# Row sums divided with 32x32 block turns on VectorE, modulations over four column tiles, and a new written order

## What is computed

```
m  = silu(cond) @ w_ada + b_ada            # nine chunks: shift, scale, gate of S, X, M
x += gS * self_attention(ln(x)*(1+scS)+shS)          # S: 16 heads of 16
x += gX * top16_cross_attention(ln(x)*(1+scX)+shX, ctx)   # X: only the 16 largest scores
x += gM * swiglu(ln(x)*(1+scM)+shM)                  # M: 256 -> 2*1024 -> 256
ss = silu(cond) @ Wss + bss                # scale and shift of L (queries) and C (context)
x += cross_attention(ada_ln(x), ada_ln(ctx)) @ Wp + bp    # L
```

## Time and profile before

| what | us |
|---|---|
| runs of the kernel before | 675.61, 676.38, 676.73 |
| the profiled execution, its time | 675.24 |
| its span, first to last instruction | 673.4 |
| TensorE busy, matmuls | 629.7 |
| TensorE busy, weight loads | 544.9 |
| VectorE busy | 454.3 |
| ScalarE busy | 438.4 |
| GpSimd busy | 340.8 |

### The profile page before, as it was taken

One profiled execution on the slowest core, in us unless ns is written; L12 is line 12 of the kernel. 1 busy time (PEld: TensorE's weight loads), 2 busy tenths in 40 slices (PEclk: granted clock), 3 DMA queues, 4 the chain that ended last, 5 costly groups with the idle time before them and its releaser, 6 DMA issues.

```text
span 673.4 us, 21451 instructions
## 1 busy us (share of the span) xinstructions
PE 629.7 (94%) x7931; PEld 544.9 (81%) x7931; DVE 454.3 (67%) x2081; ACT 438.4 (65%) x1074; POOL 340.8 (51%) x613
## 2 busy tenths in 40 slices
PE   4979977999999999999999999999999999999985
PEld 4858865888888888888988888888887877989973
DVE  2262899949948739379395694966945999953241
ACT  1446674757867766767777775776768756846553
POOL 4172242567843655746457353564742454766620
PEclk9979988999999999999999999999999999999998
DMA  9921200010110110101011101101000000000000
GB/s 289 382 85 48 74 25 26 17 49 18 33 42 18 42 33 28 45 34 41 18 41 34 40 18 34 41 17 50 17 18 18 18 25 18 3 18 9 1 10 24
DMA packets 19637, 30.32 MB, mean 45 GB/s; under 512 B 1987, under 2 KB 11087, under 8 KB 19279
## 3 DMA queue, kind: packets, MB, share of 16 engines
q1 hardware_dynamic: 19424, 28.93, 13.7%
q10 hardware_dynamic: 111, 0.03, 0.0%
HBM read 26.75 MB, written 2.20 MB: 43 GB/s over the span
## 4 chain that ended last, share of the span: by engine, by line
PE 53%; DVE 36%; SPq 4%; issue 3%; ACT 3%; DMA 1%; POOL 0%; DVEq 0%; ACTq 0%; POOLq 0%
PE dense_bank L1076 8%; DVE arena L844 8%; DVE arena L856 7%; DVE top L840 5%; PE score_room L1003 5%; DVE next L852 5%; PE dense_bank L1028 5%; PE score_room L988 5%; PE dense_bank L1065 4%; PE dense_bank L962 4%; PE dense_bank L974 3%; PE dense_bank L1050 3%; PE dense_bank L1058 3%; PE dense_bank L977 3%; PE dense_bank L1037 2%
## 5 line engine op out<-in xcount | busy, mean ns | idle before, releaser
L679 ACT ACTIVATE probs<-score_room 128x1024 f32<-128x1024 f32 x96 | 97.6, 1032 | 44.7 <-PE score_room L1009 27.7
L1076 PE MATMUL dense_bank<-h_t_M,w_m 128*128 128x128 f32 x1024 | 124.7, 277 | 1.3 <-ACT h_t_M L626 1.3
L1076 PEld LDWEIGHTS dense_bank<-h_t_M,w_m 128*128 128x128 f32 x1024 | 119.4, 192 | 4.7 <-issue 2.1
L712 ACT ACTIVATE arena<-dense_bank,bias_cols 128x128 f32<-128x128 f32 x256 | 73.3, 378 | 34.7 <-PE dense_bank L1076 34.4
L575 POOL TENSOR_SCALAR arena<-arena 128x512 bf16<-128x512 f32 x64 | 39.6, 619 | 95.1 <-DVE arena L856 94.8
L566 POOL TENSOR_TENSOR x_in<-x_in,gated 128x256 f32<-128x256 f32 x48 | 34.8, 726 | 71.8 <-DVE gated L886 71.5
L856 DVE MATCH_REPLACE8 arena<-next,arena 128x128 f32<-128x128 f32 x256 | 67.7, 276 | 0.0
L844 DVE MATCH_REPLACE8 arena<-top,arena 128x128 f32<-128x128 f32 x256 | 67.7, 276 | 0.0
L886 DVE TENSOR_TENSOR gated<-dense_bank,gates 128x256 f32<-128x256 f32 x48 | 20.0, 419 | 69.3 <-PE dense_bank L1058 41.4
L840 DVE MAX8 top<-arena 128x8 f32<-128x128 f32 x256 | 55.1, 277 | 0.9 <-ACT arena L664 0.9
L852 DVE MAX8 next<-arena 128x8 f32<-128x128 f32 x256 | 55.0, 277 | 0.0
(11 more groups left out here) (158 smaller groups left out, 1510.1 us busy)
## 6 DMA issues: line engine op xcount, KB each, us to landing
gates<-gates_dram SPq DMA_DIRECT2D x48, 256.0 KB, 3.3
x_in<-in_x SPq DMA_DIRECT2D x16, 128.0 KB, 2.2
ctx_in<-in_ctx SPq DMA_DIRECT2D x16, 128.0 KB, 2.7
w_m<-in_L_xcond_w_m SPq DMA_DIRECT2D x1, 2048.0 KB, 14.8
out_y<-x_in SPq DMA_DIRECT2D x16, 128.0 KB, 1.7
arena<-in_L_xcond_w_ada SPq DMA_DIRECT2D x2, 768.0 KB, 9.5
w_m<-in_L_xcond_w_m SPq DMA_DIRECT2D x1, 1024.0 KB, 18.6
w_qkv<-in_L_xcond_w_qkv SPq DMA_DIRECT2D x1, 768.0 KB, 5.6
```

The lines of the kernel that those rows point to most:

```text
L679: nc.scalar.activation(probs[:, pair[0], 1024 * u:1024 * u + 1024], score_room[:, 1024 * u:1024 * u + 1024], ACT.Exp).then_inc(probs_ready, 1)
L712: e = nc.scalar.activation(dst[:, P * j:P * j + P], d[:, P * j:P * j + P], ACT.Identity, bias=bias_cols[:, col + j:col + j + 1])
L1076: e = nc.tensor.matmul(d[:, P * j:P * j + P], w_m1[:, c, at:at + P], h_t["M"][:, n % H_RING["M"], c], start=(c == 0), stop=(c == CK - 1))
```

## The change

Seven edits are made together.

1. The division moves onto VectorE. `o_out`, `sumturn`, `oturn` and `o_t_out` go. `scale k` now has five instructions: a turn of the 128x512 product in 32x32 blocks from PSUM to SBUF, the reciprocals, two multiplications, and a turn of the 128x256 quotient in 32x32 blocks into `o_t`. VectorE waits for its own result between them. `out k` waits for `scale k`. The bank of `value k` is free after the first of the five.
2. The modulations swap their operands: the conditions, padded to 32 columns, are the stationary operand, and the weights are streamed, 128 columns to each of four column tiles of the array. The result has conditions on partitions, so a copy on VectorE (`mods_copy`) and a turn on TensorE (`mods_turn`) follow ahead of `mods_out`.
3. TensorE runs 24 turns of the identity before it waits for the condition.
4. ScalarE waits for the condition and computes its tanh first, then issues its nine loads.
5. TensorE turns the bias rows after `mods S`, not ahead of it; the first two setup results lie in the last two banks.
6. VectorE clears the padding of the condition at the start with one more instruction.
7. All due times are new, and with them every engine's order and the banks.

The core of the diff (the table of due times, the semaphores and the wait counters are cut):

```diff
+WARM_TURNS = 24
...
-    **{f"value {a}": f"o_out {a}" for a in ATT}, **{f"sumturn {a}": f"scale {a}" for a in ATT},
-    **{f"oturn {a}": f"o_t_out {a}" for a in ATT},
+    **{f"value {a}": f"scale {a}" for a in ATT},
...
         @block.scalar
+            act.wait_ge(cond_loaded, 16)
+            nc.scalar.activation(cond_tanh, cond, ACT.Tanh, scale=0.5).then_inc(cond_step, 1)
             at = 0
...
                 act.dma_start(bias_rows[at:at + n, :], v.rearrange("(c p) -> c p", p=P)).then_inc(rows_loaded, 16)
...
-            act.wait_ge(cond_loaded, 16)
-            nc.scalar.activation(cond_tanh, cond, ACT.Tanh, scale=0.5).then_inc(cond_step, 1)
...
+                if name == "mods_copy":
...
+                    nc.vector.tensor_copy(mod_rows[:], dense_bank[DENSE[f"mods {of[0]}", 0][0]][:, 0:P]).then_inc(mods_copied, 1)
...
                 if name == "scale":
                     k = of[0]
-                    dve.wait_ge(sums_turned, nth(f"sumturn {k}", n))
-                    nc.vector.reciprocal(iv.rearrange("p c o g -> p (c o g)"),
-                                         d[:, :, :, :, D].rearrange("p c o g -> p (c o g)")).then_inc(inv_done, 1)
+                    d = dense_bank[DENSE[f"value {k}", n][0]]
+                    dve.wait_ge(value_done, nth(f"value {k}", n))
+                    nc.vector.transpose(o_turned[:].rearrange("p j b e -> p (j b e)"), d[:]).then_inc(o_taken, 1)
+                    dve.wait_ge(o_taken, nth(full, n))
+                    nc.vector.reciprocal(inv[:].rearrange("p j b -> p (j b)"),
+                                         o_turned[:].rearrange("p j b e -> p (j b) e")[:, :, D]).then_inc(inv_done, 1)
                     dve.wait_ge(inv_done, nth(full, n))
                     for c in range(CK):
...
+                            o_norm[:, c].rearrange("p b o e -> p o b e"), o_turned[:, 2 * c:2 * c + 2, :, 0:D],
+                            inv[:, 2 * c:2 * c + 2].unsqueeze(3).broadcast_to([P, 2, GROUPS, D]), ALU.mult)
+                    e.then_inc(o_normed, 1)
+                    dve.wait_ge(o_normed, nth(full, n))
+                    if n:
+                        dve.wait_ge(out_done, nth(f"out {k}", n - 1))
+                    nc.vector.transpose(o_t[:, ATT[k]].rearrange("p c t -> p (c t)"),
+                                        o_norm[:].rearrange("p c b o e -> p (c b o e)")).then_inc(o_t_ready, 1)
...
         @block.tensor
+            def mods_of(ln, d):
...
+                for c in range(CK):
+                    for j in range(4):
+                        e = nc.tensor.matmul(d[32 * j:32 * j + 32, 0:P], silu_t[:, c], cols[j][:, c],
+                                             start=(c == 0), stop=(c == CK - 1))
...
             pe.wait_ge(ident_ready, 1)
+            for t in range(WARM_TURNS):
+                nc.tensor.transpose(dense_bank[DENSE_BANKS - 1][:, 0:P], ident[:], ident[:])
             pe.wait_ge(cond_step, 3)
...
                 if name == "mods":
...
+                    mods_of(of[0], d).then_inc(mods_done, 1)
+                    if NTH[full, 0] == 0:
+                        pe.wait_ge(rows_loaded, 9 * 16)
+                        nc.tensor.transpose(dense_bank[DENSE_BANKS - 2][:, 0:NBIAS], bias_rows,
+                                            ident[0:NBIAS, 0:NBIAS]).then_inc(setup_turned, 1)
+                if name == "mods_turn":
+                    pe.wait_ge(mods_copied, nth(f"mods_copy {of[0]}", 0))
+                    nc.tensor.transpose(d[:, 0:P], mod_rows[:], ident[:]).then_inc(mods_turned, 1)
...
-                if name == "sumturn":
...
-                if name == "oturn":
...
-                        pe.wait_ge(o_t_ready, nth(f"o_t_out {k}", n))
+                        pe.wait_ge(o_t_ready, nth(f"scale {k}", n))
```

More of the change, by code:

```diff
@@ new lines @@
+    "mods_copy S": (845,),
+    "mods_turn S": (882,),
+    "mods_out S": (940,),
+    "mods C": (1000,),
+    "mods_copy C": (1105,),
+    "mods_turn C": (1142,),
+    "mods_out C": (1187,),
+    "mods X": (2028,),
+    "mods_copy X": (2133,),
+    "mods_turn X": (2689,),
+    "mods_out X": (2965,),
+    "mods M": (2801,),
+    "mods_copy M": (2910,),
+    "mods_turn M": (2947,),
+    "mods_out M": (3046,),
+    "mods L": (3308,),
+    "mods_copy L": (3438,),
+    "mods_turn L": (3527,),
+    "mods_out L": (3572,),
@@ new lines @@
+    "gate S": (1400,),
+    "gate_out S": (1605,),
+    "gate_store S": (1732,),
+    "gate_load S": (2182, 2232, 2282, 4408, 5329, 7675, 10386, 13881, 19337, 22589, 25289, 28296, 33533, 35500, 37457, 43719),
+    "gate X": (2103,),
+    "gate_out X": (2308,),
+    "gate_store X": (2435,),
+    "gate_load X": (2885, 2935, 2985, 8344, 11608, 13669, 17488, 21872, 25836, 29089, 33473, 34126, 39930, 42390, 43808, 49199),
+    "gate M": (2460,),
+    "gate_out M": (2578,),
+    "gate_store M": (2705,),
@@ L201 @@
+    "down": (10255, 13800, 15973, 19534, 23760, 28304, 31755, 36053, 38140, 43344, 46509, 48951, 52571, 56314, 57281, 59914),
[4 rows of a table added]
 }
 ON = {
-    "pe": ("mods", "gate", "outbias", "turn", "q", "kv", "score", "maxturn", "weigh", "value", "sumturn",
-           "oturn", "down", "out", "up"),
-    "dve": ("mods_out", "gate_out", "outbias_out", "stats", "rowmax", "split", "top", "rest", "scale", "gated"),
-    "act": ("mod", "q_out", "kv_out", "score_out", "max_out", "exp", "o_out", "o_t_out", "lin", "tanh", "lin_b"),
+    "pe": ("mods", "mods_turn", "gate", "outbias", "turn", "q", "kv", "score", "maxturn", "weigh", "value",
+           "down", "out", "up"),
@@ L207 @@
+    "dve": ("mods_copy", "mods_out", "gate_out", "outbias_out", "stats", "rowmax", "split", "top", "rest", "scale", "gated"),
+    "act": ("mod", "q_out", "kv_out", "score_out", "max_out", "exp", "lin", "tanh", "lin_b"),
     "pool": ("rstd", "norm", "pre", "add", "mask", "half", "silu", "glu"),
@@ L240 @@
 DENSE = rooms({
-    **{f"mods {ln}": f"mods_out {ln}" for ln in LNS}, **{f"gate {k}": f"gate_out {k}" for k in GATE},
+    **{f"mods {ln}": f"mods_copy {ln}" for ln in LNS}, **{f"mods_turn {ln}": f"mods_out {ln}" for ln in LNS},
+    **{f"gate {k}": f"gate_out {k}" for k in GATE},
     "outbias L": "outbias_out L", **{f"turn {ln}": f"mod {ln}" for ln in LNS},
@@ L373, in block_kernel @@
         mods_done = sem("mods_done")
+        mods_copied = sem("mods_copied")
+        mods_turned = sem("mods_turned")
         mods_ready = sem("mods_ready")
@@ L428, in block_kernel @@
                    "lin": lin_ready, "lin_b": lin_b_ready, "exp": probs_ready, "rowmax": max_done,
-                   "score_out": scores_out, "mask": mask_ready, "o_out": o_ready, "scale": o_norm_ready,
-                   "o_t_out": o_t_ready, "value": value_done}
+                   "score_out": scores_out, "mask": mask_ready, "scale": o_taken, "mods_copy": mods_copied,
+                   "value": value_done}
         block = ctx.enter_context(nc.Block())
@@ L680, in _ @@
                                          score_room[:, 1024 * u:1024 * u + 1024], ACT.Exp).then_inc(probs_ready, 1)
-                if name == "o_out":
-                    k = of[0]
-                    d = dense_bank[DENSE[f"value {k}", n][0]]
-                    if n:
-                        act.wait_ge(sums_turned, nth(f"sumturn {k}", n - 1))
-                    act.wait_ge(value_done, nth(f"value {k}", n))
-                    nc.scalar.copy(o_raw[:, ATT[k]].rearrange("p j t -> p (j t)"), d[:]).then_inc(o_ready, 1)
-                if name == "o_t_out":
-                    k = of[0]
-                    d = dense_bank[DENSE[f"oturn {k}", n][0]]
-                    if n:
-                        act.wait_ge(out_done, nth(f"out {k}", n - 1))
-                    act.wait_ge(o_turned, nth(f"oturn {k}", n))
-                    nc.scalar.copy(o_t[:, ATT[k]].rearrange("p c t -> p (c t)"), d[:, 0:C]).then_inc(o_t_ready, 1)
                 if name in ("lin", "lin_b"):
@@ L766, in _ @@
                 full = " ".join(part)
+                if name == "mods_copy":
+                    if NTH[full, 0]:
+                        dve.wait_ge(mods_turned, NTH[full, 0])
+                    dve.wait_ge(mods_done, nth(f"mods {of[0]}", 0))
+                    nc.vector.tensor_copy(mod_rows[:], dense_bank[DENSE[f"mods {of[0]}", 0][0]][:, 0:P]).then_inc(mods_copied, 1)
                 if name == "mods_out":
@@ L906, in _ @@
                     wait_empty(pe, DENSE[full, n])
+                    if DENSE[full, n][1] is None and DENSE[full, n][0] >= DENSE_BANKS - 2:
+                        pe.wait_ge(cols_ready, 1)
                 if (full, n) in SCORES:
@@ L909, in _ @@
                 if name == "mods":
-                    ln = of[0]
-                    pe.wait_ge(ada_loaded[ln], 16)
-                    if ln in "LC":
-                        w = ss_q if ln == "L" else ss_kv
-                        cols = [w[:, :, P * c:P * c + P] for c in range(4)]
-                    else:
-                        at = 3 * C * MOD[ln]
```

(22 more changed lines are left out.)

67 lines of the change are left out of this document (34 added, 33 removed), and 257 rows, old and new, of the table DUE.

## The result

The changed kernel takes 669.66 us (median of 8 runs, 667.88 to 674.82) against 676.48 (8 runs, 674.64 to 679.41): a ratio of 0.991, 95% interval 0.9885 to 0.9935. That is 0.9% faster where 5.4% was forecast; the time lies at the upper edge of the range. The profiled execution took 667.88 us with a span of 665.7.

The account below looks back on a forecast made before the run. TensorE was taken to set the pace mostly, with VectorE a good third of the path. Span 673.4 - 32 - 4 - 2 + 6 - 2 - 2 = 637.4 us, plus 1.8 and 1.1, gave 640 us; range 612 to 670.

Parts of the forecast that it names:

- The prices: Expected busy times: block turns near 0.69 and 0.42 us, VectorE near 507 us, ScalarE near 392, weight loads near 500.
- The rival of two passes: VectorE's block turns take two passes over the data: 107 us added, 691 us in all, chance 0.10.
- The covered case is by far the commoner, so I take 6 us.: Of the 53 us that the division adds to VectorE, most falls in its idle time and 6 us lengthen the path.
- The bound that the prediction set aside, 28 us: VectorE's added 53 us counted by its share of the chain, 53% of its busy time, put 28 us on the path.
- VectorE is half the path: Rival: all VectorE's added time counts by its share of the chain, 28 us in place of 6: 662 us, chance 0.18.
- That is 48 x 0.66 = 32 us. I take 32.: TensorE loses `sumturn` and `oturn`, 48 times each, 0.43 and 0.23 us from start to start: 32 us saved.
- Its effect has no row; I give it nothing: The new written order of all engines was put at nothing, with plus or minus 12 us in the range.
- at most -6 for the modulations: TensorE's cheaper product for the modulations, outside the start, was to save 4 us, bounds 0 and 6.
- ScalarE, 2 us in the prediction: ScalarE loses the copies `o_out` and `o_t_out`, 46.5 us busy, of which 5% was counted on the path: 2 us saved.
- The start, a gain of 2: Cheaper first modulations and a full-pace first `q S`, against later bias rows: 2 us gained, bounds 5 gained and 3 lost.
- The tail, 2 us: At the end of the run, the chain from last `value` to `out` shortens from 3.5 to 1.8 us: 2 us gained.
- the prediction gave this even odds: Rival at the start: the 24 turns don't raise the clock, so each case ends 3 us later; chance 1 in 2.

## Why the prediction was wrong, step by step

The direction and the bookkeeping of busy time held. The steps from busy time to path did not, and a term that was put at nothing was large. That the time still lies inside the range is luck: the errors partly cancel.

- *The prices.* Block turns at 0.706 and 0.446 us, ScalarE at 398.2 us (392 expected), the modulations' groups at 3.7 us (3), weight loads at 510.3 (500). VectorE came to 518.5, not 507; 9 us of the difference are the multiplications (32.3 us against 23.4). The rival of two passes is out.
- *"The covered case is by far the commoner, so I take 6 us."* This step failed. The 219 us without work are not cover: VectorE runs its steps in a written order, and what is put into it delays the steps behind it, for which TensorE waits (`maxturn` above all). The kernel before paid 26.2 us for 51.6 that no step depended on. The bound that the prediction set aside, 28 us, was the right price, and the rival "VectorE is half the path" was right on this point.
- *"That is 48 x 0.66 = 32 us. I take 32."* The size of the work was right, the price too high: 32 us of TensorE were worth 20.3 when they were added. By the weight loads (the rule of the Trainium skill that the prediction weighed, "Perfetto Trace Analysis", the section on the most-contended engine) 33.0 us were to go, and 34.6 went, with the modulations' saving and the 24 new turns in it; the trace agrees on the work, but the time does not follow it. One rate was used for the saving (1.0) and another for the addition (0.11), where the runs show 0.63 and 0.51.
- *"Its effect has no row; I give it nothing."* With the measured rates the edits come to -20 for TensorE, at most -6 for the modulations and 64.2 x 0.51 = +33 for VectorE: 7 us slower or more, not faster (ScalarE, 2 us in the prediction, was not tried). The changed kernel is 7 us faster, so by the rates some 14 us are left over for the rest of the edits, in which the new order is the large one. By the experiments in the old order more is left: the division alone is 30 to 46 us slower there, so the rest, with 6 us for the modulations taken off, is worth 706.4 - 6 - 669.7 = 31 us to 721.4 - 6 - 669.7 = 46 us. The two estimates disagree because the rates would make the division alone only 58.1 x 0.51 - 20.3 = 9 us slower in the old order: they don't hold for a change that also moves where VectorE stands and waits. Either way the order was no spread around zero, and it gave back much of what the first two steps had wrong. No run has the old steps of the division in the new order, so what the order is worth without the division stays open.
- *The start, a gain of 2.* It was none: the first projection came 2.8 us later and TensorE had a hole of 6.3 us. I can't put a price on them: no run moved the projection (it came at 19.82 us where 16 was expected), and the hole, once moved, cost as much elsewhere. VectorE's wait of 13.30 us for a tile and DMA busy throughout (share 1.09 and 0.97 in the two stretches shown) fit a start bound by what is loaded, but no run here tried it with less to load.
- *The tail, 2 us.* The chain came out at 2.2 us where 1.8 was expected and 3.5 was before: the last `value` ends at 658.51 and its `out` starts at 660.72.

```profile
656.57 1.94 PE L1037 MATMUL dense_bank<-probs,v_one_L 128*32 128x128 f32 x32 [2.19 <-ACT probs L680]
...
660.72 2.05 PE L1062 MATMUL dense_bank<-l_p,o_t 128*128 128x256 f32 x4 [2.22 <-DVE o_t L869]
```

But `out` takes 2.05 us there, against 1.10 before, at a granted clock of 0.50 from 656 us to the end (0.96 over the last 9.4 us before), so that most of it is given back: 7.5 us from the end of the last `value` to the end of the span before (665.89 to 673.4), 7.2 after.

What stays open: that each engine's time counts for about half in both orders is shown as a rate only, and the waits were followed on TensorE alone. And part of the loss in the old order may be the clock: a mean of 0.950 over 721.5 us is 36 us' worth of full clock not granted, against 9 before (0.013 x 673.4). How much of that lies on the path wasn't separated. The runs of one kernel give a hint: the changed kernel took 667.88 us at 0.974 and 674.82 at 0.963, some 7 us more for some 8 us of full clock not granted. But a lower clock can also follow from TensorE's waits, so neither is shown to be the cause of the other.

## What to carry to other kernels

Where two engines share the chain, a first price for work that is added to one of them is its share of the chain over its share of busy time, and the same goes for work that is taken from the other; idle time on an engine with a fixed order is no cover. It is a rough price. In the kernel before it gave 0.53 for VectorE (measured 0.51) and 0.56 for TensorE (0.63); in the changed kernel 0.65 for VectorE (0.42 and 0.86) and 0.30 for TensorE, where 0.50 was measured. A change that moves work between engines has to be costed together with the order it runs in: here the division alone was 4 to 7% slower, and with an order laid out for it and the other edits 1% faster. Before the operands of a frequent VectorE operation are put in SBUF, see what GpSimd does at that time; leaving one of them in PSUM was worth 4.6 us here.

## What the hardware showed beyond that

**Multiplying two SBUF operands on VectorE takes at times nearly five times as long.** One line's instructions (ns, minimum, median, maximum), of the changed kernel and of the one with the reciprocals in PSUM:

```profile
L862 DVE TENSOR_TENSOR o_norm<-o_turned,inv x96: 276/291/1359, 53.0 to 659.8; 128x128 f32<-128x128 f32 x96
```

```profile
L862 DVE TENSOR_TENSOR o_norm<-o_turned,dense_bank x96: 279/284/290, 52.6 to 657.7; 128x128 f32<-128x128 f32 x96
```

Most take 0.29 us, some up to 1.36; with one operand in PSUM the tail is gone, and GpSimd too is busy for less (340.8 us against 344.7). The Trainium skill ("SBUF — State Buffer", the section on the two separate sides) states that a VectorE operation with two SBUF inputs and a GpSimd operation that reads SBUF shut each other out for the whole instruction. The trace agrees: 17 of the 96 take 0.43 us or more (the rest at most 0.30), each of them began while a GpSimd operation was running, and each ended 0.13 to 0.15 us behind the end of one. One of them, the first of two multiplications merged in this row, ran from 397.58 to 398.81 us, and the GpSimd operation ended at 398.66:

```profile
397.40 1.27 POOL L585 TENSOR_TENSOR arena<-arena 128x512 f32<-128x512 f32 x1
...
397.58 1.43 DVE L862 TENSOR_TENSOR o_norm<-o_turned,inv 128x128 f32<-128x128 f32 x2
```

The prediction had taken these multiplications over at their old price.

**Turns of the identity do raise TensorE's pace.** 16 records of the modulations take 0.65 us behind 24 turns and 1.08 without them; without them another 16 still take 1.08 at 13.39 us, so it isn't the time that has passed. The Trainium skill ("TensorE: Matmul & The Clock Gate", Part 4) states that TensorE's transpose mode does not engage the full clock, as it doesn't count as busy time in the same way; the prediction gave this even odds, and here the trace disagrees. What the turns bought did not last. TensorE had nothing to do from the end of the first modulations to 10.07 us, and the granted clock stood at 0.54 from 9 to 17 us, the lower of the two levels (1.2 GHz) for most of that time; the first projection, at 20.12 us, still ran at half pace.

**A recorded clock of 1.00 is not full pace before the first change of the record.** The stretch from 9 to 17 us of the kernel without the turns, and a step in it:

```profile
9.00:17.00 8.00, 3.79 (x23) 1.73 (x24) 3.55 (x20) 0.00 (x0) 0.46 (x3) 1.00 1.09 338
```

```profile
13.39 1.08 PE L900 MATMUL dense_bank<-arena,silu_t 128*32 128x128 f32 x16
```

The granted clock is recorded as 1.00, yet the modulations of C take 1.08 us, and the first `q S` of the kernel before took 2.06 us at 1.00 as well. Durations tell the pace at the start of a trace, the record doesn't.
